# Attention values in one stationary block of high and low rows, halves added by VectorE; maximum as bias of one sequence's exponentials

## The chip, the cores and the metric

The kernel runs on one core of one Trainium2 chip. The metric is the device time of one execution in microseconds (us). The engines are TensorE (PE; its weight loads are PEld), VectorE (DVE), ScalarE (ACT), GpSimd (POOL) and SyncE (SP), which here issues the transfers. Each engine runs its own queue in order; they wait for each other by semaphores.

## The reference, cut to what matters

```python
# x: 32 sequences of 64 tokens, 1024 wide; 32 query heads, 8 key and value heads, 32 wide
x = x + attn(cond(x))          # cond: linear layer with a low-rank term chosen by labeler
x = x + ffn(cond2(x))          # two linear layers with routed low-rank terms
# in attn, for each sequence:
q, k, v = split(x @ w_qkv.T + b_qkv)
q, k = rope(q), rope(k)
scores = where(causal, q @ k.T / sqrt(32), -1e20)
out = softmax(scores) @ v      # this product is what the change is about
out = out @ w_o.T + b_o
```

## The kernel before, in words

The time has five stages: weights of the first two layers are folded into one (up to about 150 us), attention over all tokens (to about 610 us), folding for the second half, the output projection, and the feed-forward layers. The change is in the attention stage.

Products are made in fp32r, a rounded fp32, and every factor is split into a high part and a low remainder; a product is then high x high, high x low and low x high, three passes. ScalarE makes the high parts (`*_h`), VectorE or GpSimd the low parts (`*_l`).

Attention works on 16 units of 128 tokens, two sequences b = 0 and 1 of 64 tokens each. It is a pipeline of three: in step u TensorE projects unit u to q, k and v, makes the scores of unit v = u - 1, and multiplies probabilities and values of unit w = u - 2. `steps` writes steps 0 and 1 out, then a loop over u = 2 to 14, then steps 15, 16 (no projection any more) and 17 (values only). In step 16 the place of the projection is taken by `fold2.first(k)`, the first products of the next stage, each of which needs one more row of weights; ScalarE makes the high row (L1145), VectorE or GpSimd the low row (L1151). In step 17, `last_values`, it is `fold2.second`.

A step's projection is 24 groups (k, part), k = 0 to 7 and part = 0 to 2. Ahead of each group, the table `BESIDE` names work of the older units: `transpose_p` (probabilities turned, L952), `attend` (values, L967), `transpose_qk` (q and k turned, L924) and `scores` (L937). At the end the down product of the low-rank term is scaled by VectorE (`low_down`, L774), turned (L978), and split (L670, L849), and `up` (L984) adds it; behind `up` VectorE writes `qkv` (L860) and the next step begins.

On VectorE a step is: `probs_low` of sequence 0 (L745), four operations of the rotation (L740, two behind `rot_re`, two behind `rot_im`; GpSimd finishes each pair, L706 and L708), the low part of the values (L791), `probs_low` of sequence 1, low parts of q and k (L749, L810), values into their blocks (L820), and for each sequence mask, maximum and subtraction (`less_max`, L828, L830, L832). ScalarE makes the exponentials: 16 small ones with their sums for sequence 0 (L613), one large for sequence 1 (L615), which VectorE sums (L760). GpSimd scales them (L697). The scores of sequence 0 stand in PSUM banks 4 and 5 (`s_ps`), those of sequence 1 in banks 6 and 7 (`t_ps`), which the turned tiles use as well.

In `attend` one stationary tile is the block of four value heads, 128 columns, with zeros for the two heads that do not belong to the moving probabilities; high and low values are two tiles, `vb_h` and `vb_l`. Each sequence has a bank of its own for the result, and ScalarE copies it to `attn` (`values_out`, L601):

```python
for vv, pp in ((vb_h, pt_h), (vb_l, pt_h), (vb_h, pt_l)):
    if pp is pt_l:
        pe.wait_ge(pt_low, 2 * v + b + 1)
    for q in range(QUADS):
        for j in range(2):
            mm = pe.matmul(s_ps[:, b, ...], vv[:, b, q, j, :, :], pp[:, q, j, :, :], ...)   # 128 x 256
```

Of the kernel before, what the change touches and what calls it, by code (L numbers as in the profile page):

```python
# [22 lines left out]
ALU = mybir.AluOpType  # L23
# [416 lines left out]
def attention(nc, a, sem, keep, psum, ring, c_h, a_raw, index, fold1, fold2):  # L440
# [21 lines left out]
    vb_h, vb_l = (sb(n, [P, BPU, QUADS, 2, 4, HD], F32R) for n in ("vb_h", "vb_l"))  # L462
# [27 lines left out]
    v_high, v_low, vb_zero, vb_high, vb_low = (sem(n) for n in ("v_high", "v_low", "vb_zero", "vb_high", "vb_low"))  # L490
# [14 lines left out]
    def diag(vb, b, h):  # L505

        flat = vb[h * SEQ:(h + 1) * SEQ, b, :, :, :, :].rearrange("p q j c d -> p q (j c d)")
        return flat.rearrange("p q (m d) -> p q m d", d=HD)[:, :, h:h + 7:6, :]
# [83 lines left out]
    def scalar(act):  # L592
# [14 lines left out]
        def exp_scores(v, b, sums):  # L607

            act.wait_ge(s_sub, 2 * v + b + 1)
            if sums:  # L610
                for g in range(2):
                    for c in range(KVH):
                        last = act.activation(prob[:, 0, g, c, :], prob[:, 0, g, c, :], ACT.Exp, scale=SCALE, accum_out=ssum[:, 0, g, c:c + 1])  # L613
            else:
                last = act.activation(prob[:, b, :, :, :], prob[:, b, :, :, :], ACT.Exp, scale=SCALE)  # L615
            last.then_inc(s_exp, 1)

        def step(u, main, score, value, nxt):
# [6 lines left out]
            if value:  # L625
# [5 lines left out]
                values_out(w, 0)  # L631
# [4 lines left out]
                values_out(w, 1)  # L636
            if score:
# [12 lines left out]
                act.wait_ge(vb_zero, 2)  # L650
                need(act, pv_done, 2 * v)
                for b in range(BPU):
                    for h in range(2):
                        last = act.activation(diag(vb_h, b, h), v_hl[b * SEQ:(b + 1) * SEQ, 0, :, :, h, :].bitcast(F32), ACT.Copy)
# [29 lines left out]
    def gpsimd(pool):  # L684
# [46 lines left out]
        pool.memset(vb_h[:, :, :, :, :, :].bitcast(F32), 0.0).then_inc(vb_zero, 1)  # L731
        pool.memset(vb_l[:, :, :, :, :, :].bitcast(F32), 0.0).then_inc(vb_zero, 1)
        steps(pool, step)

    def vector(dve):
        def rotate(v, part):

            pairs = qkv[:, 0:QK].rearrange("p (h i two) -> p h i two", i=HD // 2, two=2)
            for n, (dst, table) in enumerate(((roped[:, :, :, part], (cos, sin)[part]), (rot_t[:, part, :, :], (sin, cos)[part]))):
                last = dve.tensor_tensor(dst, pairs[:, :, :, n], table[:, :].unsqueeze(1).to_broadcast([P, NH, HD // 2]), ALU.mult)  # L740
            last.then_inc((rot_re, rot_im)[part], 1)
# [1416 lines left out]
```

## Time and profile before

| | |
|---|---|
| median of 3 runs | 1169.55 us (1167.64 to 1171.43) |
| the profiled execution | 1169.91 us, span 1168.1 us |
| TensorE busy | 1140.2 us, 98% of the span |
| VectorE busy | 684.0 us, 59% |
| ScalarE busy | 409.5 us, 35% |
| GpSimd busy | 206.8 us, 18% |
| granted TensorE clock, mean | 0.994 of full speed |

The time of an execution is its span in the profile and a little around it. Busy shares are means over all stages; what counts for the change is the attention stage, and in it the order in which one step's waits end. Matmuls are pipelined: the start of one and of the next tell the pace, the duration shown for one is longer.

### The profile page before, as it was taken

What the parts mean: (1) busy time and instruction counts of PE and PEld (TensorE: products, weight loads), DVE (VectorE), ACT (ScalarE), POOL (GpSimd) and SP (SyncE); (2) the same over time, 40 slices, a digit from 0 to 9 for tenths busy, and PEclk for the clock granted to TensorE, in tenths of its full rate; (3) what the DMA queues carried; (4) which work ended last, traced back from release to release, by engine and by line L of the source; (5) the groups of instructions that cost most, each with busy time, mean ns of one, the idle gap of its engine ahead of it and who ended that gap; (6) DMA issues with size and microseconds to landing.
All of it is one profiled execution on the core that took longest, in us unless ns stands there. A gap on an engine that the chain in (4) does not pass through costs nothing.

```text
span 1168.1 us, 16980 instructions
## 1 busy us (share of the span) xinstructions
PE 1140.2 (98%) x6176; PEld 996.5 (85%) x6176; DVE 684.0 (59%) x1197; ACT 409.5 (35%) x1173; POOL 206.8 (18%) x133
## 2 busy tenths in 40 slices
PE   8999999999999999999988999999999999999998
PEld 6888888888888888888888999788888788888886
DVE  5312147788888888888893334332136766667664
ACT  5312124555555555555553333111123322222221
POOL 0000124333343333444361000000000000000000
PEclk9999999999999999999989999999999999999999
DMA  8020032111111111111142114473561333322212
GB/s 286 15 64 19 10 117 67 46 57 51 45 45 51 48 45 45 45 45 36 39 147 90 56 37 159 130 215 101 153 180 57 106 109 109 109 108 99 80 57 90
DMA packets 89763, 98.30 MB, mean 84 GB/s; under 512 B 7666, under 2 KB 73842, under 8 KB 89714
## 3 DMA queue, kind: packets, MB, share of 16 engines
q1 hardware_dynamic: 89714, 97.64, 25.8%
q8 instruction: 32, 0.52, 0.2%
q14 instruction: 17, 0.14, 0.0%
HBM read 72.45 MB, written 25.17 MB: 84 GB/s over the span
## 4 chain that ended last, share of the span: by engine, by line
PE 92%; DVE 3%; DMA 2%; ACT 1%; POOL 1%; issue 1%; SPq 0%; DVEq 0%; POOLq 0%
PE psum L905 23%; PE psum L1541 14%; PE psum L1849 13%; PE psum L280 12%; PE psum L1281 9%; PE psum L967 4%; PE psum L1910 4%; PE psum L1829 4%; PE psum L937 4%; PE psum L952 2%; PE psum L924 2%; PE psum L984 1%; DVE low L774 1%; DMA raw<-x_t_scratch 1%; PE psum L1896 0%
## 5 line engine op out<-in xcount | busy, mean ns | idle before, releaser
L905 PE MATMUL psum<-p_h,c_high_low 128*128 128x512 f32 (+1 forms) x768 | 196.3, 359 | 0.5 <-DVE qkv L860 0.5
L905 PEld LDWEIGHTS psum<-p_h,c_high_low 128*128 128x128 f32 x768 | 133.6, 188 | 13.3 <-issue 0.7
L280 PE MATMUL psum<-c_high_low,w_h 128*128 128x512 f32 x384 | 120.4, 399 | 5.7 <-ACT w_h L345 5.7
L1541 PE MATMUL psum<-ring,rows 128*128 128x512 f32 x528 | 123.7, 392 | 1.2 <-DVE t_plain L1257 1.2
L1541 PEld LDWEIGHTS psum<-ring,rows 128*128 128x128 f32 x528 | 98.8, 188 | 24.1 <-DVE t_plain L1257 2.5
L1281 PE MATMUL psum<-chunk,rows 128*128 128x384 f32 (+1 forms) x576 | 110.2, 347 | 4.8 <-DVE rows L1151 2.5
L1281 PEld LDWEIGHTS psum<-chunk,rows 128*128 128x128 f32 x576 | 104.3, 194 | 5.4 <-issue 5.4
L905 PE MATMUL psum<-p_l,c_high_low 128*128 128x512 f32 (+1 forms) x384 | 104.2, 366 | 0.0
L280 PEld LDWEIGHTS psum<-c_high_low,w_h 128*128 128x128 f32 x384 | 74.0, 193 | 22.5 <-issue 5.6
L697 POOL TENSOR_TENSOR prob<-prob,sinv 128x1024 f32<-128x1024 f32 x32 | 61.9, 1935 | 125.2 <-DVE sinv L767 125.2
L687 POOL TENSOR_TENSOR c_high_low<-ring_plain,c_high_low 128x512 fp32r<-128x512 f32 x32 | 41.4, 1292 | 236.6 <-PE psum L280 139.9
L613 ACT ACTIVATE prob<-prob 128x64 f32<-128x64 f32 x240 | 57.8, 242 | 67.6 <-DVE prob L832 67.6
L905 PE MATMUL psum<-end_h,c_high_low 128*128 128x320 f32 x256 | 76.1, 310 | 0.0
L280 PE MATMUL psum<-c_high_low,w_l 128*128 128x512 f32 x192 | 73.9, 391 | 0.0
L905 PEld LDWEIGHTS psum<-p_l,c_high_low 128*128 128x128 f32 x384 | 66.5, 190 | 6.2
L1849 PE MATMUL psum<-t_high,s_blocks 128*128 128x512 f32 x192 | 65.8, 405 | 0.0
L266 DVE TENSOR_TENSOR p_l<-psum,p_h 128x512 fp32r<-128x512 f32 (+1 forms) x24 | 14.2, 602 | 83.5 <-ACT p_h L254 42.7
L1501 DVE TENSOR_TENSOR ring<-ring_plain,ring 128x512 fp32r<-128x512 f32 x22 | 15.2, 690 | 74.8 <-ACT ring L1496 74.8
L1541 PE MATMUL psum<-at,rows 128*128 128x512 f32 x240 | 56.5, 391 | 0.0
L905 PEld LDWEIGHTS psum<-end_h,c_high_low 128*128 128x128 f32 x256 | 47.0, 188 | 8.6
L1541 PEld LDWEIGHTS psum<-at,rows 128*128 128x128 f32 x240 | 45.0, 188 | 9.8
L601 ACT ACTIVATE ring_plain<-psum 128x512 f32<-128x512 f32 x32 | 19.3, 603 | 89.4 <-PE psum L967 89.4
(173 smaller groups left out, 2261.4 us busy)
## 6 DMA issues: line engine op xcount, KB each, us to landing
ring_plain<-in_x_t SPq DMA_DIRECT2D x32, 256.0 KB, 2.7
attn_scratch<-ring_plain SPq DMA_DIRECT2D x16, 512.0 KB, 2.7
ring_plain<-attn_scratch SPq DMA_DIRECT2D x32, 256.0 KB, 4.0
raw<-x_t_scratch SPq DMA_DIRECT2D x16, 512.0 KB, 4.1
rest<-in_b_base SPq DMA_DIRECT2D x16, 512.0 KB, 4.1
out<-rest SPq DMA_DIRECT2D x16, 512.0 KB, 2.6
ring_plain<-in_wqkv_t SPq DMA_DIRECT2D x10, 512.0 KB, 6.1
a_raw<-in_lora_a SPq DMA_DIRECT2D x32, 128.0 KB, 2.0
```

The costliest lines, as they stand in the source:

```text
L280: mm = pe.matmul(to, stationary, moving, start=k == 0 and m == 0, stop=k == KT - 1 and last, skip_group_check=True)
L613: last = act.activation(prob[:, 0, g, c, :], prob[:, 0, g, c, :], ACT.Exp, scale=SCALE, accum_out=ssum[:, 0, g, c:c + 1])
L687: pool.tensor_tensor(x_l[:, ks(half), :], x_raw[:, ks(half), :], x_h[:, ks(half), :].bitcast(F32), ALU.subtract).then_inc(x_low, 1)
L697: pool.tensor_tensor(rows, rows, sinv[:, b, :, :].rearrange("p g c -> p (g c)").unsqueeze(2).to_broadcast([P, 2 * KVH, SEQ]), ALU.mult).th ...
L905: mm = pe.matmul(to, sx[:, k, :], moving(w, n, k), start=first, stop=False, skip_group_check=True)
L937: mm = pe.matmul(o, qq[:, b, cols, :].rearrange("p g t -> p (g t)"), kk[:, q, b, :, :].rearrange("p c t -> p (c t)"), start=n == 0, stop=n ...
L967: mm = pe.matmul(s_ps[:, b, q * 4 * SEQ:(q + 1) * 4 * SEQ], vv[:, b, q, j, :, :].rearrange("p c d -> p (c d)"), pp[:, q, j, :, :].rearrang ...
L1281: mm = pe.matmul(self.tile(n, width), stationary, moving, start=k == 0 and m == 0, stop=k == KT - 1 and m == 2, skip_group_check=True)
L1541: mm = pe.matmul(self.psum[:, self.BANK_OF[i], :], w[:, cols], s, start=m == 0 and p == 0, stop=m == KT - 1 and p == 2, skip_group_check=True)
L1829: mm = pe.matmul(self.gate_ps[:, u, :], s[:, k % HALF, :], self.room.gates[:, m, k, :], start=k == 0 and n == 0, stop=k == KT - 1 and n == ...
L1849: mm = pe.matmul(self.banks[self.BANK_OF[name]], s[:, k, :], w[:, k, :], start=name in ("p1", "p5", "p6") and k == 0 and n == 0, stop=k == ...
L1910: mm = pe.matmul(self.banks[{"c11": "a", "c12": "c", "c21": "b", "c22": "d"}[name]], self.zt[:, r, s, u, :], w[m], start=name == "c22" and ...
```

## The change

Values: one tile `vb` holds, for each group of two heads, 64 columns of high values and 64 of low ones. One pass with all 128 columns over `pt_h` writes high x high to PSUM rows 0 to 63 and low x high to rows 64 to 127; a second pass with the 64 high columns over `pt_l` adds to rows 0 to 63. No zero blocks for the other pair of heads are multiplied any more. ScalarE copies rows 64 to 127 to `beside`, and VectorE adds them to rows 0 to 63 and writes `attn`, in two operations, rows 0 to 63 and rows 64 to 127. The result now takes both banks of `s_ps`, so `attend` of sequence 1 waits for `pv_out` of sequence 0. Places: `values_out` stands on VectorE behind the third operation of the rotation, with `probs_low` of sequence 1 and then the fourth behind it; the second `values_out` ahead of the low parts of q and k.

Exponentials: in the full steps the maximum of sequence 0 is not subtracted by VectorE; it is multiplied by -SCALE (128 x 16) and given to ScalarE's exponentials as bias.

`BESIDE`: `transpose_qk` goes from (2, 1) to (3, 0) and from (3, 1) to (3, 2), `scores` from (4, 0) and (5, 0) to (4, 2) and (5, 2).

```diff
-    vb_h, vb_l = (sb(n, [P, BPU, QUADS, 2, 4, HD], F32R) for n in ("vb_h", "vb_l"))
+    vb = sb("vb", [P, BPU, QUADS, 2, 2, 2, HD], F32R)
+    beside = sb("beside", [SEQ, QUADS, 2, GRP * SEQ])
...
+    def values(rows):
+
+        return s_ps[rows, :, :].rearrange("p q (j t) -> p q j t", j=2)
+
+    high_rows, low_rows = slice(0, SEQ), slice(SEQ, P)
...
-        def values_out(w, b):
+        def values_beside(w, b):
             act.wait_ge(pv_done, 2 * w + b + 1)
-            if b == 0:
-                need(act, stored, 16 * w)
-            act.activation(attn[:, :, b, :], s_ps[:, b, :].rearrange("p (k t) -> p k t", k=KT), ACT.Copy).then_inc(pv_out, 1)
+            need(act, pv_out, 2 * w + b)
+            act.activation(beside[:, :, :, :], values(low_rows), ACT.Copy).then_inc(pv_beside, 1)
...
-                        last = act.activation(prob[:, 0, g, c, :], prob[:, 0, g, c, :], ACT.Exp, scale=SCALE, accum_out=ssum[:, 0, g, c:c + 1])
+                        last = act.activation(prob[:, 0, g, c, :], prob[:, 0, g, c, :], ACT.Exp, scale=SCALE, bias=smax[:, 0, g, c:c + 1],
+                                              accum_out=ssum[:, 0, g, c:c + 1])
...
+        def values_out(w, b):
+            dve.wait_ge(pv_beside, 2 * w + b + 1)
+            if b == 0:
+                need(dve, stored, 16 * w)
+            for j in range(2):
+                to = attn[j * SEQ:(j + 1) * SEQ, :, b, :].rearrange("p (q g) t -> p q g t", q=QUADS)
+                one, two = (t[:, :, j, :].rearrange("p q (g t) -> p q g t", g=GRP) for t in (values(high_rows), beside[:, :, :, :]))
+                last = dve.tensor_tensor(to, one, two, ALU.add)
+            last.then_inc(pv_out, 1)
...
-                rotate(v, 1)
+                rotate(v, 1, (0,))
+                if value:
+                    values_out(w, 0)
+                    probs_low(w, 1)
+                rotate(v, 1, (1,))
...
+            if value and not score:
+                values_out(w, 0)
+                probs_low(w, 1)
             if value:
-                probs_low(w, 1)
+                values_out(w, 1)
...
+                    if main and b == 0:
+                        dve.tensor_scalar(row(smax, b), row(smax, b), -SCALE, None, ALU.mult).then_inc(s_sub, 1)
+                        return
                     dve.tensor_tensor(flat(b), flat(b), row(smax, b).unsqueeze(2).to_broadcast([P, 2 * KVH, SEQ]), ALU.subtract).then_inc(s_sub, 1)
...
-            for vv, pp in ((vb_h, pt_h), (vb_l, pt_h), (vb_h, pt_l)):
+            else:
+                pe.wait_ge(pv_out, 2 * v + 1)
+            for parts, pp in ((2, pt_h), (1, pt_l)):
                 if pp is pt_l:
                     pe.wait_ge(pt_low, 2 * v + b + 1)
                 for q in range(QUADS):
                     for j in range(2):
+                        v_at = vb[:, b, q, j, 0:parts, :, :].rearrange("p m h d -> p (m h d)")
+                        mm = pe.matmul(s_ps[0:parts * SEQ, q, j * GRP * SEQ:(j + 1) * GRP * SEQ], v_at, pp[:, q, j, :, :].rearrange("p g t -> p (g t)"),
+                                       start=parts == 2 and j == 0, stop=parts == 1 and j == 1, skip_group_check=True)
...
-                  (2, 1): [(attend, 2, 1), (transpose_qk, 1, (0, 1))], (3, 1): [(transpose_qk, 1, (2,))],
+                  (2, 1): [(attend, 2, 1)], (3, 0): [(transpose_qk, 1, (0, 1))], (3, 2): [(transpose_qk, 1, (2,))],
```

What stands where, at three places. First VectorE in a full step, from `probs_low` of sequence 0 to the low parts of q, before the change (`pt_l`: low probabilities; `roped`, `rot_t`: rotation; `v_hl`: values; the names behind "waits" are semaphores):

```order
L745 TENSOR_TENSOR pt_l<-psum,pt_h 128x1024 [waits pt_high]
L740 TENSOR_TENSOR roped<-qkv,cos 128x640 [waits rotated,qk_t,const_in,qkv_out]
L740 TENSOR_TENSOR rot_t<-qkv,sin 128x640
L740 TENSOR_TENSOR roped<-qkv,sin 128x640
L740 TENSOR_TENSOR rot_t<-qkv,cos 128x640
L791 TENSOR_TENSOR v_hl<-qkv,v_hl 128x256 [waits v_high]
L745 TENSOR_TENSOR pt_l<-psum,pt_h 128x1024 [waits pt_high]
L749 TENSOR_TENSOR q_l<-psum,q_h 128x2x2x64 [waits qk_high]
```

The same place after the change, line numbers of the changed kernel (`ring_plain` is where `attn` lies):

```order
L753 TENSOR_TENSOR pt_l<-psum,pt_h 128x1024 [waits pt_high]
L747 TENSOR_TENSOR roped<-qkv,cos 128x640 [waits rotated,qk_t,const_in,qkv_out]
L747 TENSOR_TENSOR rot_t<-qkv,sin 128x640
L747 TENSOR_TENSOR roped<-qkv,sin 128x640
L763 TENSOR_TENSOR ring_plain<-psum,beside 64x8x64 [waits attn_stored,pv_beside]
L763 TENSOR_TENSOR ring_plain<-psum,beside 64x8x64
L753 TENSOR_TENSOR pt_l<-psum,pt_h 128x1024 [waits pt_high]
L747 TENSOR_TENSOR rot_t<-qkv,cos 128x640
L813 TENSOR_TENSOR v_hl<-qkv,v_hl 128x256 [waits v_high]
L763 TENSOR_TENSOR ring_plain<-psum,beside 64x8x64 [waits pv_beside]
L763 TENSOR_TENSOR ring_plain<-psum,beside 64x8x64
L767 TENSOR_TENSOR q_l<-psum,q_h 128x2x2x64 [waits qk_high]
```

The fourth operation of the rotation has moved behind two adds and the second `probs_low`, and two more adds stand ahead of `q_l`.

Second, TensorE in step 16, from the second `attend` to the second turn of q and k, before the change (L1281: products of the next stage):

```order
L967 MATMUL psum<-pt_h,vb_h 128x256 [waits pt_high]
L967 MATMUL psum<-pt_h,vb_h 128x256 x3
L967 MATMUL psum<-pt_h,vb_l 128x256 x4
L967 MATMUL psum<-pt_l,vb_h 128x256 [waits pt_low]
L967 MATMUL psum<-pt_l,vb_h 128x256 x3
L924 MATMUL psum<-ident,roped 128x128 [waits pt_low,rotated]
L924 MATMUL psum<-ident,roped 128x128 x7
L1281 MATMUL psum<-chunk,rows 128x392 [waits f2_row_low,f2_chunk_low]
L1281 MATMUL psum<-chunk,rows 128x392 x11
L924 MATMUL psum<-ident,roped 128x128 [waits qk_low]
```

And after it:

```order
L997 MATMUL psum<-pt_h,vb 128x256 [waits pv_out,pt_high]
L997 MATMUL psum<-pt_h,vb 128x256 x3
L997 MATMUL psum<-pt_l,vb 64x256 [waits pt_low]
L997 MATMUL psum<-pt_l,vb 64x256 x3
L1310 MATMUL psum<-chunk,rows 128x392 [waits f2_row_low,f2_chunk_low]
L1310 MATMUL psum<-chunk,rows 128x392 x11
L952 MATMUL psum<-ident,roped 128x128 [waits pt_low,rotated]
L952 MATMUL psum<-ident,roped 128x128 x7
L952 MATMUL psum<-ident,roped 128x128 [waits qk_low]
L952 MATMUL psum<-ident,roped 128x128
```

Both turns of q and k have moved behind the products that need the third row of weights.

Third, VectorE in step 16 behind the values' low part (`v_hl`), where the third and fourth rows of weights are split, before the change:

```order
L791 TENSOR_TENSOR v_hl<-qkv,v_hl 128x256 [waits v_high]
L745 TENSOR_TENSOR pt_l<-psum,pt_h 128x1024 [waits pt_high]
L1151 TENSOR_TENSOR rows<-rows_plain,rows 128x1024 [waits f2_row_low,f2_row_high]
L1151 TENSOR_TENSOR rows<-rows_plain,rows 128x1024 [waits f2_row_high]
L749 TENSOR_TENSOR q_l<-psum,q_h 128x2x2x64 [waits qk_high]
```

And after it:

```order
L813 TENSOR_TENSOR v_hl<-qkv,v_hl 128x256 [waits v_high]
L763 TENSOR_TENSOR ring_plain<-psum,beside 64x8x64 [waits pv_beside]
L763 TENSOR_TENSOR ring_plain<-psum,beside 64x8x64
L1180 TENSOR_TENSOR rows<-rows_plain,rows 128x1024 [waits f2_row_low,f2_row_high]
L1180 TENSOR_TENSOR rows<-rows_plain,rows 128x1024 [waits f2_row_high]
L767 TENSOR_TENSOR q_l<-psum,q_h 128x2x2x64 [waits qk_high]
```

The rows of weights now stand behind the adds of the second sequence. On ScalarE the copy for these adds stands behind the high parts of the same two rows, as `values_out` did.

## Rows read from the trace of the kernel before

**Rows 1.** Busy windows, core 0: length, busy time and count by engine, granted clock, DMA.

```profile
200.00:560.00 360.00, 357.21 (x2285) 321.67 (x2284) 294.69 (x431) 191.05 (x704) 149.34 (x92) 1.00 0.13 46
```

**Rows 2.** Timeline of TensorE, one step: start, duration, line, tiles, count, idle before.

```profile
305.60 1.03 PE L952 MATMUL psum<-ident,prob 128*128 128x128 f32 x8
...
308.65 0.64 PE L967 MATMUL psum<-pt_h,vb_h 128*128 128x256 f32 x4
309.12 0.63 PE L967 MATMUL psum<-pt_h,vb_l 128*128 128x256 f32 x4
...
315.39 1.04 PE L924 MATMUL psum<-ident,roped 128*128 128x128 f32 x8
...
320.13 0.28 PE L937 MATMUL psum<-k_h,q_h 128*128 128x256 f32 x1
...
323.76 0.27 PE L937 MATMUL psum<-k_h,q_h 128*128 128x256 f32 x1
...
332.40 0.98 PE L984 MATMUL psum<-pb,lows 128*128 128x512 f32 x4
333.22 1.04 PE L952 MATMUL psum<-ident,prob 128*128 128x128 f32 x8
```

**Rows 3.** Timeline of VectorE, the same step.

```profile
305.33 1.89 DVE L860 TENSOR_TENSOR qkv<-psum,b_bc 128x512 f32<-128x512 f32 x3 [0.30 <-PE psum L984]
...
310.34 0.82 DVE L740 TENSOR_TENSOR roped<-qkv,sin 128x640 f32<-128x640 f32 x1
311.07 2.23 DVE L740 TENSOR_TENSOR rot_t<-qkv,cos 128x640 f32<-128x640 f32 x1
...
313.56 1.21 DVE L745 TENSOR_TENSOR pt_l<-psum,pt_h 128x1024 fp32r<-128x1024 f32 x1
...
321.77 1.22 DVE L828 TENSOR_TENSOR prob<-psum,hidden 128x1024 f32<-128x1024 f32 x1 [1.06 <-PE psum L937]
...
330.19 0.59 DVE L774 TENSOR_SCALAR low<-psum 64x128 f32<-64x128 f32 x2 [0.42 <-PE psum L905]
330.81 1.22 DVE L760 TENSOR_REDUCE ssum<-prob 128x16 f32<-128x1024 f32 x1
```

**Rows 4.** Timeline of ScalarE and GpSimd, the same step.

```profile
310.35 0.60 ACT L601 ACTIVATE ring_plain<-psum 128x512 f32<-128x512 f32 x1 [2.35 <-PE psum L967]
310.50 2.12 POOL L706 TENSOR_TENSOR roped<-roped,rot_t 128x640 f32<-128x640 f32 x1 [1.59 <-DVE rot_t L740]
...
311.14 1.03 ACT L605 ACTIVATE pt_h<-psum 128x1024 fp32r<-128x1024 f32 x1 [0.19 <-PE psum L952]
...
313.38 1.71 POOL L708 TENSOR_TENSOR roped<-roped,rot_t 128x640 f32<-128x640 f32 x1 [0.76 <-DVE rot_t L740]
...
325.54 0.26 ACT L613 ACTIVATE prob<-prob 128x64 f32<-128x64 f32 x1 [4.46 <-DVE prob L832]
...
329.39 1.04 ACT L615 ACTIVATE prob<-prob 128x1024 f32<-128x1024 f32 x1
```

**Rows 5.** Timeline of step 16, each engine's rows in order of time.

```profile
584.82 3.93 PE L1281 MATMUL psum<-chunk,rows 128*128 128x392 f32 x12 [1.97 <-DVE rows L1151]
588.58 0.63 PE L967 MATMUL psum<-pt_h,vb_h 128*128 128x256 f32 x4
...
593.33 2.63 DVE L1151 TENSOR_TENSOR rows<-rows_plain,rows 128x1024 fp32r<-128x1024 f32 x2
...
594.43 1.04 PE L924 MATMUL psum<-ident,roped 128*128 128x128 f32 x8
...
595.13 0.38 ACT L640 ACTIVATE keys<-psum 128x256 f32<-128x256 f32 x1
595.23 2.40 PE L1281 MATMUL psum<-chunk,rows 128*128 128x392 f32 x12
...
608.10 6.60 PE L1281 MATMUL psum<-chunk,rows 128*128 128x392 f32 x27 [2.38 <-POOL rows L1151]
```

**Rows 6.** Busy window behind the first wait of step 16, core 0.

```profile
584.80:588.60 3.80, 3.79 (x13) 3.80 (x14) 3.80 (x3) 0.36 (x1) 2.41 (x1) 0.55 0.97 320
```

More of the change, by code:

```diff
@@ L630, in step @@
                         fold2.copy_out(act, i, 0, i)
-                values_out(w, 0)
+                values_beside(w, 0)
                 probs_high(w, 1)
@@ L635, in step @@
                     fold2.high_row(act, 3)
-                values_out(w, 1)
+                values_beside(w, 1)
             if score:
@@ L653, in step @@
                     for h in range(2):
-                        last = act.activation(diag(vb_h, b, h), v_hl[b * SEQ:(b + 1) * SEQ, 0, :, :, h, :].bitcast(F32), ACT.Copy)
+                        last = act.activation(diag(0, b, h), v_hl[b * SEQ:(b + 1) * SEQ, 0, :, :, h, :].bitcast(F32), ACT.Copy)
                 last.then_inc(vb_high, 1)
@@ L730, in gpsimd, with rotate @@
         pool.wait_ge(fold1.done, fold1.TILES * fold1.STEPS)
-        pool.memset(vb_h[:, :, :, :, :, :].bitcast(F32), 0.0).then_inc(vb_zero, 1)
-        pool.memset(vb_l[:, :, :, :, :, :].bitcast(F32), 0.0).then_inc(vb_zero, 1)
+        pool.memset(vb[:, :, :, :, :, :, :].bitcast(F32), 0.0).then_inc(vb_zero, 1)
         steps(pool, step)
     def vector(dve):
-        def rotate(v, part):
+        def rotate(v, part, which=(0, 1)):
             pairs = qkv[:, 0:QK].rearrange("p (h i two) -> p h i two", i=HD // 2, two=2)
             for n, (dst, table) in enumerate(((roped[:, :, :, part], (cos, sin)[part]), (rot_t[:, part, :, :], (sin, cos)[part]))):
+                if n not in which:
+                    continue
                 last = dve.tensor_tensor(dst, pairs[:, :, :, n], table[:, :].unsqueeze(1).to_broadcast([P, NH, HD // 2]), ALU.mult)
-            last.then_inc((rot_re, rot_im)[part], 1)
+            if 1 in which:
+                last.then_inc((rot_re, rot_im)[part], 1)
         def probs_low(w, b):
@@ L819, in step @@
                     for h in range(2):
-                        last = dve.tensor_copy(diag(vb_l, b, h), v_hl[b * SEQ:(b + 1) * SEQ, 1, :, :, h, :].bitcast(F32))
+                        last = dve.tensor_copy(diag(1, b, h), v_hl[b * SEQ:(b + 1) * SEQ, 1, :, :, h, :].bitcast(F32))
                 last.then_inc(vb_low, 1)
@@ L966, in attend @@
                     for j in range(2):
-                        mm = pe.matmul(s_ps[:, b, q * 4 * SEQ:(q + 1) * 4 * SEQ], vv[:, b, q, j, :, :].rearrange("p c d -> p (c d)"),
-                                       pp[:, q, j, :, :].rearrange("p g t -> p (g t)"), start=n == 0, stop=pp is pt_l and j == 1, skip_group_check=True)
-                        n += 1
+                        v_at = vb[:, b, q, j, 0:parts, :, :].rearrange("p m h d -> p (m h d)")
+                        mm = pe.matmul(s_ps[0:parts * SEQ, q, j * GRP * SEQ:(j + 1) * GRP * SEQ], v_at, pp[:, q, j, :, :].rearrange("p g t -> p (g t)"),
+                                       start=parts == 2 and j == 0, stop=parts == 1 and j == 1, skip_group_check=True)
             mm.then_inc(pv_done, 1)
```

14 lines of the change are left out of this document (6 added, 8 removed).

## The prediction

> **What bounds the kernel now.** I read the busy windows first: from 200 to 560 us, the loop over units, TensorE is busy 357.2 of 360 us at full granted clock, VectorE 294.7 [rows 1]. So TensorE sets the pace, with little room: anything it loses there is added to the time, but what it gains counts only as far as the other engines keep up. Then the timeline of one step. TensorE starts the transposes of the probabilities at 305.60 and again at 333.22: a step takes 27.62 us [rows 2]. All times below with a plus sign are counted from that start. At the end of the step stands a chain over other engines: second scores at 323.76, `less_max`, exponentials, the sum at 330.81, `lows`, and `up` at 332.40 [rows 2, 3]. There are 14 such steps (13 turns of the loop and step 15). One more place matters, step 16, where attention of the last units stands beside the first products of the next stage; there TensorE waits 2.0 and 2.4 us for rows of weights [rows 5].
>
> **What the change removes on TensorE.** Each `attend` has 12 matmuls of 256 columns now, 8 afterwards. Four of them follow each other in 0.47 us (308.65 to 309.12), so 0.119 each and 0.48 less per `attend` [rows 2]. 32 of these are 15.2 us, the most that there is to gain. The second pass has only 64 stationary columns, but streams the same 256 columns; I give it no gain.
>
> **What it adds in a step, first half.** The Scalar copy now takes 64 rows by 1024 columns from PSUM. The nearest row, 128 by 1024 from PSUM, took 1.03 us, the old copy 0.60 [rows 4]. The old copy began 1.70 after the first matmul of `attend` (308.65 to 310.35); with 0.48 less it begins at +4.27 and ends at +5.30. VectorE is free for the adds at +5.47, where the fourth rotation started (311.07) [rows 3], so the copy is just covered. Each add is 64 by 512 with one operand in PSUM. Three such operations of 128 by 512 took 1.89 us, which is 0.685 for one and 0.60 from start to start [rows 3]. The two 64-row operations of `low_down`, which write the lower rows and then the upper, took 0.59 together, double one: no overlap there [rows 3]. I take that for the adds too: 2 x 0.695 = 1.39 us, and the adds end at +6.86.
>
> The Trainium skill, page "VectorE: DVE Perf Modes", section on two Vector instructions with no wait between them, says the same as a rule: an instruction whose output starts in another group of 32 partitions starts only when all earlier ones are finished. By the overlapped spacing the sum would be 0.1 to 0.2 us less in a step; the `low_down` row agrees with the page.
>
> Then `probs_low` (1.14 to the next start, from 1.21 less the overlap) ends its place at +8.00. Now the fourth rotation. In the kernel before it takes 2.23 us against 0.82 for its three sisters, because GpSimd's addition (310.50, 2.12 us) runs beside it: it ends at 313.30, 0.68 after GpSimd's end at 312.62 [rows 3, 4]. `probs_low`, which reads PSUM, ran beside GpSimd at 313.56 undisturbed. So the adds fill the 1.4 us that were lost, and the moved rotation takes 0.82: end at +8.82. GpSimd's second addition ended 1.79 after the end of the rotation (315.09 against 313.30), so `rotated` comes at +10.61, and TensorE may go on at about +10.66. In the kernel before it was at the q and k transposes at +9.79.
>
> TensorE itself arrives there at 9.79 - 2 x 0.48 - 0.09 (it waited a moment for `pt_l` at the third pass) + 1.46 for the two groups of projection now ahead of it, that is +10.20; a group is about 0.73, from the three between the score blocks, 3.63 less 1.43 for the block itself. So it waits 0.46. The gain of 0.95 is already half gone, and the transposes start 0.87 later than before.
>
> **Second half of the step.** From these transposes to the first scores five groups and one small turn lie as before (315.39 to 320.13), and three groups between the score blocks as before (to 323.76): 8.37 together [rows 2]. The second scores start at 10.66 + 8.37 = +19.03; before +18.16. From there a chain runs that TensorE cannot shorten. VectorE starts on scores 1.64 after their first matmul (320.13 to 321.77). Mask, maximum and subtraction lead to the exponentials 3.77 later (321.77 to 325.54); these take 1.04 for the second sequence, which keeps its subtraction; 0.03 on, the sum starts, and from the sum to `up` it is 1.59 (330.81 to 332.40); `up` to the next step is 0.82 [rows 2 to 4]. Sum: 1.64 + 3.77 + 1.07 + 1.59 + 0.82 = 8.89. The step becomes 19.03 + 8.89 = 27.92, **0.30 longer** than 27.62.
>
> Why did this chain not bind before? It would give 18.16 + 8.89 = 27.05, under 27.62: VectorE was late for another reason, the subtraction for sequence 0 (about 1.2, as the mask of the same size) in front of mask 1, and `low_down` waiting for TensorE's last group. The change removes that subtraction: a 128 by 16 operation of about 0.25 (from the reciprocal of that size) stands there. But the second scores are two groups nearer the end of the step, so VectorE waits for TensorE about 0.8 us in front of mask 1 (the blocks are 3.63 apart, mask, maximum and the small operation take 2.8), and what was removed only lengthens this wait. The bias is read from SBUF by 16 exponentials that start later than before only by neighbours' shifts and end a microsecond ahead of need; cost nil, and if each took 0.06 more, 0.2 us of the step. 14 steps: **+4.2 us**. Bounds: if `rotated` is no limit, TensorE goes on at +10.20, the step is 27.46 and the term -2.2; if each add takes 0.82 like a rotation and the biased exponentials their 0.2, it is about +0.6 a step, +8.4.
>
> **Step 16.** `attend` 0 starts at 588.58. Copy from 589.80 to 590.83, adds to 592.25, `probs_low` to 593.47, then four matmuls: `attend` 1 is over at 594.05. In the kernel before VectorE was on the low row of weights 2 at 593.33, straight behind `probs_low` [rows 5]. Now `values_out` of sequence 1 stands ahead of it: copy 594.32 to 595.35, adds to 596.77, row 2 (1.2 to 1.3) to 598.0. TensorE's third row of products, at 595.23 before, starts at 598.1, having done nothing for 4.0 us. Ahead of it the q and k transposes were done; now they stand behind. And the clock: before, TensorE waited 1.97 us in its queue and the granted clock then was 0.55 of full over 584.8 to 588.6; twelve matmuls took 3.93 us there, 2.40 at 595.23 [rows 5, 6]. I expect the level of 1.2 GHz again behind the 4.0 us: end of the twelve about 601.85. Then the transposes, and the copy to `keys` 0.70 behind their start (594.43 to 595.13): 602.55 against 595.13, **+7.4 us**.
>
> The Trainium skill, page "TensorE: Matmul & The Clock Gate", Part 1, holds that an idle TensorE falls to 1.2 GHz and only activity frees the clock; the granted 0.55 agrees. Without that fall this term would be 5.9.
>
> From `keys` everything follows in queue order on ScalarE (queries, keys, values, row 4, three chunks, three rows) and behind it on GpSimd, for whose rows TensorE waited 2.38 us at 608.10 [rows 5]. There is no slack in between, so the end of step 16 moves by the same 7.4. Also both q and k turns now meet at k = 3 with nothing between: the last turn waits for `q_l`, about 1.1 us, inside these 7.4. In step 17 VectorE and GpSimd set the first `attend`; the second saves 0.48. Bounds for steps 16 and 17: 4 (no clock fall, a little shadow) to 8.
>
> **The sum** on the profiled execution, 1169.9 us (span 1168.1, the rest around it): +4.2 + 7.4 - 0.5 = 1181.0. The median of the runs is 0.4 below that execution, so I predict **1180.5 us**.
>
> **Rivals.**
> 1. *TensorE stays the bound* (chance 8 in 100, the one on the other side). If the chain behind the second scores were shorter than TensorE's own work there (1.43 + seven groups' worth and the rest, some 6.6 us to `up`, against 8.07 for the chain), and `rotated` 0.46 earlier, each step would save up to 0.95: -13.3. With 4 to 7 us lost in step 16 that is 1160 to 1163 us. It decides at a chain 1.4 us shorter; for it speaks TensorE's 99%, against it every duration in the chain.
> 2. *Only step 16 loses* (17 in 100): the adds are quicker than I think or start to start 0.60, `rotated` comes in time, the loop is between -0.16 and +0.1 a step: about 1174.5.
> 3. *Step 16 absorbs its delay* (10 in 100): the weight rows are made in idle time elsewhere and only the loop's 4.2 are left, or a small part of the 7.4: 1173.
> 4. *VectorE's queue is worse than walked* (7 in 100): adds slowed beside GpSimd, +0.6 or more a step: 1186 to 1190.
> My own case holds 58 in 100, 1176 to 1185.
>
> **Numbers.** A change under 0.3% (3.5 us) is what a measurement of this kernel can hardly tell from none. Slower than 1173.1 holds my case, rival 4, and most of 2 and half of 3: 0.78. Same, 1166 to 1173: 0.13. Faster: 0.09. The range 1171 to 1186 leaves out rival 1, a part of 4 and the low ends of 2 and 3, under 2 in 10.
>
> **What would show it.** In the profile after: `attend` of 8 matmuls in 0.95 us; the rotation that took 2.23 at 0.82; TensorE waiting for GpSimd's `roped` about 0.5 in each step; mask 1 waiting about 0.8 for the scores; TensorE waiting near 1.0 us for `low` and 0.5 for `lows`; steps of 27.9. In step 16 a wait of about 4 us ahead of the third row of products with a granted clock near 0.55 behind it. I am wrong if the steps take under 27.5, which would say that the chain at their end is shorter than my sum, or if the third row of products starts without that wait.

## The result, and the profile of the changed kernel

| | before | after | predicted |
|---|---|---|---|
| median | 1169.28 us (1167.64 to 1171.43, 4 runs) | 1196.33 us (1192.86 to 1196.87, 4 runs) | 1180.5 us, 1171 to 1186 |
| profiled span | 1168.1 us | 1194.1 us | |
| one step of the loop | 27.62 us | 29.01 us in the mean, 28.60 in most | 27.92 us |
| step 16, start of the transposes to the next | 34.55 us | 40.94 us | 7.4 us more |

The changed kernel is slower, ratio 1.0222 (1.0202 to 1.0242). The direction was right. The size was not: 27.1 us where 11.1 were predicted (1181.0 less 1169.9), above the range's end.

First the busy window of the loop and that of the stretch with step 16 (length, busy time and instructions of PE, PEld, DVE, ACT and POOL, granted clock, share and rate of DMA):

```profile
200.00:560.00 360.00, 334.98 (x2081) 298.25 (x2081) 284.96 (x463) 210.78 (x663) 140.20 (x86) 0.99 0.13 45
600.00:650.00 50.00, 34.69 (x191) 31.58 (x190) 37.43 (x52) 24.66 (x44) 25.02 (x13) 0.88 0.28 97
```

Before, TensorE was busy 357.2 of 360 us [rows 1]. Now it is 335.0, and no other engine is near full: the loop has become a chain through several engines. The granted clock of the loop is 0.99 where it was 1.00.

The timeline of TensorE in one step, from 253.71 to 282.31, so 28.60 us:

```profile
253.71 1.03 PE L980 MATMUL psum<-ident,prob 128*128 128x128 f32 x8
256.76 0.63 PE L997 MATMUL psum<-pt_h,vb 128*128 128x256 f32 x4
257.22 0.63 PE L997 MATMUL psum<-pt_l,vb 128*64 128x256 f32 x4
257.69 1.04 PE L980 MATMUL psum<-ident,prob 128*128 128x128 f32 x8
...
264.38 1.09 PE L952 MATMUL psum<-ident,roped 128*128 128x128 f32 x8 [0.35 <-POOL roped L714]
...
272.79 0.27 PE L965 MATMUL psum<-k_h,q_h 128*128 128x256 f32 x1
...
279.87 0.30 PE L1007 MATMUL psum<-ident,low 128*128 128x128 f32 x1 [1.57 <-DVE low L792]
281.51 0.97 PE L1013 MATMUL psum<-pb,lows 128*128 128x512 f32 x4 [0.17 <-DVE lows L877]
282.31 1.04 PE L980 MATMUL psum<-ident,prob 128*128 128x128 f32 x8
```

Read against [rows 2] from the start of each step: the q and k transposes stand at +10.67 (before +9.79), the second scores at +19.08 (+18.16). I had predicted +10.66 and +19.03. So two thirds of the step went as walked. The rest did not: TensorE waits 1.57 us for `low`, where 1.0 was predicted.

VectorE in the same step:

```profile
259.18 1.38 DVE L763 TENSOR_TENSOR ring_plain<-psum,beside 64x512 f32<-64x512 f32 x2
260.59 1.23 DVE L753 TENSOR_TENSOR pt_l<-psum,pt_h 128x1024 fp32r<-128x1024 f32 x1
261.73 0.82 DVE L747 TENSOR_TENSOR rot_t<-qkv,cos 128x640 f32<-128x640 f32 x1
...
273.31 0.17 DVE L858 TENSOR_SCALAR smax<-smax 128x16 f32<-128x16 f32 x1
274.41 1.22 DVE L853 TENSOR_TENSOR prob<-psum,hidden 128x1024 f32<-128x1024 f32 x1 [0.93 <-PE psum L965]
275.67 1.22 DVE L855 TENSOR_REDUCE smax<-prob 128x16 f32<-128x1024 f32 x1
276.92 1.23 DVE L860 TENSOR_TENSOR prob<-prob,smax 128x1024 f32<-128x1024 f32 x1
278.96 0.25 DVE L785 RECIPROCAL sinv<-ssum 128x16 f32<-128x16 f32 x1 [0.82 <-ACT prob L618]
279.13 0.59 DVE L792 TENSOR_SCALAR low<-psum 64x128 f32<-64x128 f32 x2
279.91 1.22 DVE L778 TENSOR_REDUCE ssum<-prob 128x16 f32<-128x1024 f32 x1 [0.19 <-ACT prob L621]
```

The second subtraction ends at 278.15, and then VectorE waits 0.82 us for the exponentials of sequence 0. That wait is what the prediction did not have. ScalarE shows why:

```profile
273.52 0.35 ACT L618 ACTIVATE prob<-prob,smax 128x64 f32<-128x64 f32 x1 [3.62 <-DVE smax L858]
...
278.84 1.04 ACT L621 ACTIVATE prob<-prob 128x1024 f32<-128x1024 f32 x1
```

The 16 exponentials fill 273.52 to 278.84, 5.32 us. In the kernel before, 325.54 to 329.39 is 3.85 [rows 4]. The group of all 240 of them, in the page of costliest groups, gives the price of one:

```profile
L618 ACT ACTIVATE prob<-prob,smax 128x64 f32<-128x64 f32 x240 | 80.0, 335 | 55.1 <-DVE smax L858 55.1
```

It was 242 ns before, so 0.093 us more for each, 1.5 for 16. By the predicted walk the exponential of sequence 1 would start at 19.03 + 1.64 + 3.77 = +24.44; it starts at +25.13. From there to the next step it is 3.47 us, and 3.48 had been predicted.

Step 16, each engine's rows in order of time:

```profile
604.69 2.36 PE L1310 MATMUL psum<-chunk,rows 128*128 128x392 f32 x12 [1.96 <-DVE rows L1180]
...
614.06 1.38 DVE L763 TENSOR_TENSOR ring_plain<-psum,beside 64x512 f32<-64x512 f32 x2 [0.75 <-ACT beside L606]
615.48 2.36 DVE L1180 TENSOR_TENSOR rows<-rows_plain,rows 128x1024 fp32r<-128x1024 f32 x2
616.85 4.21 PE L1310 MATMUL psum<-chunk,rows 128*128 128x392 f32 x12 [3.88 <-DVE rows L1180]
620.89 1.04 PE L952 MATMUL psum<-ident,roped 128*128 128x128 f32 x8
621.53 0.39 ACT L646 ACTIVATE keys<-psum 128x256 f32<-128x256 f32 x1 [7.50 <-PE psum L952]
```

The wait of 3.88 us ahead of the third row of products is there (4.0 predicted), and behind it twelve matmuls take 4.21 us where full clock gives 2.40 [rows 5]. The granted clock of that stretch:

```profile
616.85:620.90 4.05, 4.05 (x13) 3.96 (x14) 0.99 (x1) 0.00 (x0) 0.00 (x0) 0.50 0.19 76
```

`keys` comes at +19.84 from the start of the step, before at +13.31, so 6.5 later.

One thing in the loop is new. In four of its steps the transposes at the start take nearly double, here with the end of the step before and with the granted clock of that stretch:

```profile
308.54 0.30 PE L1007 MATMUL psum<-ident,low 128*128 128x128 f32 x1 [1.58 <-DVE low L792]
...
310.18 1.60 PE L1013 MATMUL psum<-pb,lows 128*128 128x512 f32 x4 [0.17 <-DVE lows L877]
311.58 1.91 PE L980 MATMUL psum<-ident,prob 128*128 128x128 f32 x8
```

```profile
311.60:313.50 1.90, 1.90 (x10) 1.90 (x10) 1.25 (x3) 0.00 (x0) 1.90 (x2) 0.50 0.01 3
```

0.50 is the level of 1.2 GHz. It follows a wait of 1.58 us for `low`, but the same wait stands in every step, and only every fourth shows it. Of the fourteen steps, 195.49 to 601.69 is 406.2 us; fourteen at 28.62 would be 400.7, so these falls cost 5.5 us.

The span's 26.0 us more are thus: 14 x 0.98 = 13.7 for the undisturbed step (28.60 against 27.62), some 5.8 with the clock and rounding up to the loop's 19.5, 6.4 for step 16, 0.3 before the loop, and -0.3 behind step 16.

### The profile page after: what moved, and what is told of

It is laid out like the page before. It is cut to its first block, busy times and chain, and to the rows that moved or that the text cites. A ratio compares the mean times of both kernels' runs of the same rounds, so it can differ in the third digit from the quotient of the medians.

```text
span 1194.1 us, 16835 instructions
## 1 busy us (share of the span) xinstructions
PE 1132.9 (95%) x6048; PEld 985.0 (82%) x6048; DVE 690.8 (58%) x1261; ACT 445.3 (37%) x1173; POOL 205.2 (17%) x132
## 4 chain that ended last, share of the span: by engine, by line
PE 68%; DVE 10%; ACT 10%; POOL 5%; issue 4%; DMA 2%; SPq 0%; DVEq 0%; POOLq 0%
PE psum L1570 14%; PE psum L280 12%; PE psum L1878 12%; PE psum L1310 9%; ACT prob L618 7%; PE psum L933 7%; PE psum L1939 4%; PE psum L1858 4%; POOL roped L712 2%; POOL roped L714 2%; PE psum L965 2%; PE psum L952 2%; DVE ssum L778 2%; PE psum L980 2%; DVE prob L853 2%
## 5 line engine op out<-in xcount | busy, mean ns | idle before, releaser
L933 PE MATMUL psum<-p_h,c_high_low 128*128 128x512 f32 (+1 forms) x768 | 199.5, 363 | 0.5 <-DVE qkv L888 0.5
L933 PEld LDWEIGHTS psum<-p_h,c_high_low 128*128 128x128 f32 x768 | 133.1, 189 | 13.7 <-issue 0.7
L618 ACT ACTIVATE prob<-prob,smax 128x64 f32<-128x64 f32 x240 | 80.0, 335 | 55.1 <-DVE smax L858 55.1
L606 ACT ACTIVATE beside<-psum 64x1024 f32<-64x1024 f32 x32 | 32.8, 1025 | 70.7 <-PE psum L997 70.6
L853 DVE TENSOR_TENSOR prob<-psum,hidden 128x1024 f32<-128x1024 f32 x32 | 39.1, 1223 | 30.5 <-PE psum L965 30.5
```

The source lines that it names most:

```text
L606: act.activation(beside[:, :, :, :], values(low_rows), ACT.Copy).then_inc(pv_beside, 1)
L853: dve.tensor_tensor(flat(b), scores, hidden[:, :].unsqueeze(1).to_broadcast([P, 2 * KVH, SEQ]), ALU.add).then_inc(s_masked, 1)
L933: mm = pe.matmul(to, sx[:, k, :], moving(w, n, k), start=first, stop=False, skip_group_check=True)
```

## Experiments

One table for all of them, from the profiled executions: the mean step (transposes of the first step to those of step 16, over 14), step 16, and what lies behind it. The ratio is against runs of the kernel before that were taken side by side with the kernel in question; their median went from 1167.97 to 1169.83. The last column goes from 548.7 to 554.5, though the edits touch only its beginning, so single executions compare only to some 3 us, and the argument goes by the steps.

| kernel | median, us | ratio to before (95%) | step | step 16 | behind |
|---|---|---|---|---|---|
| before | 1169.28 | | 27.62 | 34.55 | 551.7 |
| after | 1196.33 | 1.0222 (1.0202 to 1.0242) | 29.01 | 40.94 | 551.5 |
| after, no bias | 1187.20 | 1.0148 (1.0124 to 1.0171) | 28.21 | 41.29 | 554.5 |
| before, bias alone | 1169.24 | 1.0005 (0.9992 to 1.0018) | 27.70 | 33.49 | 548.7 |
| after, old table | 1187.22 | 1.0160 (1.0137 to 1.0184) | 28.61 | 36.86 | 552.2 |
| before, constant pointer | 1187.19 | 1.0152 (1.0128 to 1.0176) | 28.75 | 34.53 | 551.7 |
| after, old step 16 | 1190.73 | 1.0198 (1.0174 to 1.0222) | 28.85 | 37.67 | 550.9 |
| after, addition on VectorE | 1187.59 | 1.0166 (1.0145 to 1.0186) | 28.16 | 41.17 | 552.3 |
| before, sum behind `lows` | 1169.71 | 1.0008 (0.9995 to 1.0021) | 27.72 | 33.90 | 548.7 |
| combination | 1172.02 | 1.0027 (1.0016 to 1.0038) | 27.72 | 37.24 | 551.1 |
| and values' low half on GpSimd | 1168.96 | 1.0008 (0.9994 to 1.0022) | 27.53 | 36.25 | 551.4 |
| and `low_down` first | 1173.28 | 1.0042 (1.0027 to 1.0057) | 27.85 | 36.78 | 551.7 |
| the same with the bias | 1173.99 | 1.0043 (1.0027 to 1.0059) | 27.85 | 36.95 | 550.6 |

My theory after the result: the pointer operand makes each exponential 0.093 us longer, so that in the side by side kernel they and not VectorE end last. The rival: the 0.7 us come from the new places in TensorE's queue or from the adds.

**After, no bias.** The subtraction of sequence 0 is back.

```diff
-prob[:, 0, g, c, :], ACT.Exp, scale=SCALE, bias=smax[:, 0, g, c:c + 1], accum_out=...
+prob[:, 0, g, c, :], ACT.Exp, scale=SCALE, accum_out=...
-                    if main and b == 0:
-                        dve.tensor_scalar(row(smax, b), row(smax, b), -SCALE, None, ALU.mult)...
-                        return
```

> The changed kernel with the maximum of sequence 0 subtracted by VectorE again and no bias. Theory (the 16 biased exponentials, 0.335 us each against 0.242, end 0.7 us after the second subtraction and hold the chain to up; the longer idle time then costs clock in every fourth step): the exponentials take 0.242, steps about 28.2 us instead of 29.0 in the mean, no step with a fallen clock, median about 1184.5 us. Rival (the exponentials are hidden, the new places of scores and of the q and k transposes cost the time): steps stay near 28.6 to 29, median 1194 to 1197.

A step takes 28.21 us, and no step shows a fallen clock. The total came out 2.7 us above the expected 1184.5, about as much as the stretch behind step 16 was longer in the profiled execution (554.5 against 551.5). VectorE and ScalarE at the end of one (it begins at 251.56):

```profile
274.84 1.23 DVE L856 TENSOR_TENSOR prob<-prob,smax 128x1024 f32<-128x1024 f32 x1
276.43 0.25 DVE L784 RECIPROCAL sinv<-ssum 128x16 f32<-128x16 f32 x1 [0.36 <-ACT prob L618]
...
276.30 1.04 ACT L620 ACTIVATE prob<-prob 128x1024 f32<-128x1024 f32 x1
```

The exponential of sequence 1 now starts at +24.74, 0.39 sooner than with the bias, and the step is 0.39 shorter. So the bias made a step longer although it takes 1.05 us from VectorE. Even here the 16 exponentials end 0.23 behind the second subtraction (276.07): they start a subtraction later, at +20.89.

**Before, bias alone.** The same edit the other way round, on the kernel before.

> The kernel before with the bias alone. Theory: the exponentials take 0.335 (1.5 us more), but the subtraction that VectorE saves (1.2 us) comes ahead of them, so in the old places the step grows only by about 0.1 us, median 1169 to 1173. Rival (the bias costs its 0.7 us a step wherever it stands): steps 28.3, median about 1179.

No difference. The exponentials take 335 ns there as well, but in a kernel whose TensorE is busy all the time the chain is covered: 0.08 us a step.

**Before, constant pointer.** The exponentials of the kernel before read a column of zeros as their bias and the subtraction stays, so that nothing is saved and only the pointer is added.

```diff
-prob[:, 0, g, c, :], ACT.Exp, scale=SCALE, accum_out=...
+prob[:, 0, g, c, :], ACT.Exp, scale=SCALE, bias=hidden[:, 0:1], accum_out=...
```

> The kernel before, subtraction kept, whose 16 exponentials read a constant column of zeros as bias (same result). Theory: it is reading a bias from SBUF at all that costs: 0.335 us each, with nothing saved on VectorE, so steps near 28.8, median about 1186 (more if the clock falls). Rival (what costs is a column just written, or another one for each exponential): 0.242 each and 1169 us.

Its group of exponentials:

```profile
L613 ACT ACTIVATE prob<-prob,hidden 128x64 f32<-128x64 f32 x240 | 79.9, 334 | 67.7 <-DVE prob L832 67.7
```

334 ns with a constant column that nobody writes in the loop: what costs is the operand, not a wait for `smax`. And 1.5 us more of exponentials make a step 1.13 longer.

The Trainium skill, page "ScalarE: Activation LUTs", in the section on what ACT_TABLE_LOAD costs, gives the same size: about 93 ns for each pointer operand of one column. The rows agree: 242 ns without, 334 and 335 with.

**After, old table.** TensorE's queue has the table of before.

> The changed kernel with the table of places of before. Theory: the chain from the rotation to the first scores sets the loop, so TensorE waits about 1.9 us at the q and k transposes instead of 0.5 there, and steps stay near 28.6; step 16 gives back about 6 us; median 1185 to 1191, by whether the clock still falls. Rival (the places are what costs in the loop): steps near 27.7, median below 1178.

The step is 28.61, the undisturbed step of the changed kernel: apart from the falls of the clock the places in the table are worth nothing in the loop. TensorE waits elsewhere:

```profile
263.57 1.09 PE L952 MATMUL psum<-ident,roped 128*128 128x128 f32 x8 [1.79 <-POOL roped L714]
279.17 0.30 PE L1007 MATMUL psum<-ident,low 128*128 128x128 f32 x1 [0.20 <-DVE low L792]
```

1.79 us for GpSimd's `roped` and 0.20 for `low`, where it was 0.35 and 1.57; the sum is nearly the same, 1.99 and 1.92. The chain through the other engines sets the step, wherever in it TensorE stands and waits. With this split the clock does not fall in the loop. That, and step 16, 4.1 us shorter (6 expected), is why the total is 9 us less. Step 16 of this run, where only TensorE's table is the old one and VectorE still makes the addition ahead of row 2:

```profile
609.34 1.97 PE L952 MATMUL psum<-ident,roped 128*128 128x128 f32 x8 [1.81 <-POOL roped L714]
610.03 2.36 DVE L1180 TENSOR_TENSOR rows<-rows_plain,rows 128x1024 fp32r<-128x1024 f32 x2
611.40 2.94 PE L1310 MATMUL psum<-chunk,rows 128*128 128x392 f32 x12
```

While VectorE adds and then makes row 2, TensorE waits for `roped` and turns q and k, and no wait of 3.9 us is left.

**After, old step 16.** The old table and the old order of VectorE, rows of weights 2 and 3 ahead of the addition of sequence 1, in step 16 alone.

```diff
-            if value:
+            if value and (main or not score):
                 values_out(w, 1)
             if score and not main:
                 fold2.low_row(dve, 2, after_other=True)
                 fold2.low_row(dve, 3)
+                values_out(w, 1)
```

> The changed kernel, with the old order of step 16 alone put back: there the old table of TensorE's queue, and the rows of weights 2 and 3 on VectorE ahead of the addition of the halves of sequence 1. My theory (the addition in front of row 2 makes TensorE wait 3.9 us and run twelve matmuls at the low clock): step 16 loses its 6 to 7 us, total 1189 to 1191. Rival (step 16 is longer for what its own attends and additions cost, wherever they stand): 1194 to 1196.

The total came out at 1190.7 as expected, but not for the reason given. Step 16 gained 3.3 us, half of what I gave it, and less than the 4.1 of the old table alone; 2.3 came from the loop, where two steps show a fallen clock at their start instead of four. What is left of step 16:

```profile
612.05 1.97 PE L953 MATMUL psum<-ident,roped 128*128 128x128 f32 x8 [1.81 <-POOL roped L714]
613.67 4.27 PE L1314 MATMUL psum<-chunk,rows 128*128 128x392 f32 x12
```

The transposes start 0.5 later than before (+13.10 against +12.61), but behind a wait of 1.81 us that was not there, and they and the twelve matmuls take 1.97 and 4.27 us instead of 1.04 and 2.40. So in the old places `roped`, late by the adds, costs a fall of the clock as well. Set beside the run with the old table, VectorE's old order gained nothing: the twelve matmuls start 1.62 behind the transposes instead of 2.06, but take 4.27 instead of 2.94, because the clock came back later. The old order of VectorE with the new table was not run.

**After, addition on VectorE.** GpSimd's second addition of the rotation is moved to VectorE.

```diff
-                pool.wait_ge(rot_im, v + 1)
-                pool.tensor_tensor(roped[:, :, :, 1], roped[:, :, :, 1], rot_t[:, 1, :, :], ALU.add)...
+                dve.wait_ge(rot_im, v + 1)
+                dve.tensor_tensor(roped[:, :, :, 1], roped[:, :, :, 1], rot_t[:, 1, :, :], ALU.add)...
```

> The changed kernel, with the second addition of the rotation (1.8 us on GpSimd) done by VectorE, about 0.8 us there. My theory (in the first half of a step TensorE waits for GpSimd's addition, and its delay is carried to the end of the step): rotated comes about 1 us earlier, TensorE's wait for it goes, a step takes 28.1 to 28.2 instead of 28.6, total 1189 to 1191, and 1184 to 1186 if the falls of the clock go too. Rival (VectorE has no room, and what GpSimd loses VectorE pays): no change, 1195 to 1198.

It takes 0.83 us there, and TensorE comes to the transposes at +10.21 without a wait, the +10.20 predicted for its own arrival. The step is 28.16 in the mean and 28.13 in most; the clock of the profiled execution is low only at the start of the first step (eight transposes in 1.45, step 28.54), though TensorE still waits 1.57 us for `low` in each step. The total lies between the two values expected.

**Before, sum behind `lows`.** The kernel before with the sum of sequence 1 one place later in VectorE's queue.

> The kernel before, with only the sum for sequence 1 moved behind the low halves of the values in VectorE's queue. Theory: TensorE is the bound there, the chain at the end of its step is nearly hidden, so a step gains at most 0.1 us: 1167.5 to 1169.3. Rival (the end chain bound before, too): steps of 27.0 to 27.2, 1161 to 1164.

Nothing is gained (27.72 a step): the end chain is hidden in the kernel before, as the prediction had it.

**The combination.** No bias, the addition on VectorE, the sum behind `lows`, the old step 16, on the changed kernel.

> Side by side without the bias (all subtractions back), the second addition of the rotation on VectorE, the sum for sequence 1 moved behind the low halves of the values (lows) in VectorE's queue, and the old order in step 16. If the places named so far are all that keeps the 8-matmul attends from paying, a step takes 27.3 to 27.4 and the total is 1163 to 1167, below the kernel before. Rival (TensorE's own 27.1 or so a step cannot be reached, the end chain stays as it is): steps of 27.7 to 27.9 and 1170 to 1174.

27.72 a step: the rival was right, and the reason is VectorE, busy 321.4 us of the window 200 to 560 where it was 294.7 [rows 1].

```profile
322.71 1.22 DVE L853 TENSOR_TENSOR prob<-psum,hidden 128x1024 f32<-128x1024 f32 x1 [1.14 <-PE psum L961]
...
328.88 1.23 DVE L857 TENSOR_TENSOR prob<-prob,smax 128x1024 f32<-128x1024 f32 x1
330.46 0.25 DVE L782 RECIPROCAL sinv<-ssum 128x16 f32<-128x16 f32 x1 [0.36 <-ACT prob L618]
330.64 0.59 DVE L789 TENSOR_SCALAR low<-psum 64x128 f32<-64x128 f32 x2
```

From the first mask (322.71) to the next step (333.39) is a chain of 10.7 us, six operations of VectorE in a row first. What TensorE saves cannot shorten it. Against the undisturbed 28.60 the step is 0.88 shorter, and the two edits measured alone, the bias (0.39) and the addition on VectorE (0.47), give 0.86 of that: the place of the sum gave nothing that can be seen.

**Values' low half on GpSimd.** One more operation off VectorE, and the scores one group earlier.

> The last combination (no bias, second addition of the rotation on VectorE, sum for sequence 1 behind lows, old order in step 16) with the low half of the values (one subtraction of 0.42 us) moved from VectorE to GpSimd, which is idle for 8.9 us there, and both score blocks one group of projection (0.73 us) earlier on TensorE. Theory: in the last combination a step of 27.73 is set by the scores, by six VectorE operations behind them (7.4 us without a gap) and by the chain to up; then the step follows the scores: 27.0 to 27.1, total 1162 to 1165, below the kernel before. Rival: the operands of the first scores (k_l, q_l) are not ready earlier, or GpSimd's subtraction holds VectorE up as its addition did: steps of 27.4 to 27.7, 1168 to 1172.

Only 0.2 us of the 0.7 came: the scores, at +15.14 instead of +15.39, wait for `q_l`, which VectorE ends late.

```profile
319.83 0.39 PE L961 MATMUL psum<-k_h,q_h 128*128 128x256 f32 x1 [0.28 <-DVE q_l L767]
```

This is the best of the side by side kernels, and it is level with the kernel before, 1.0008 (0.9994 to 1.0022).

**`low_down` first, and the same with the bias.** `low_down` stands ahead of the reciprocal of sequence 0.

> The kernel of the run before (steps of 27.52 us), with low_down ahead of the reciprocal of sequence 0 in VectorE's queue, so that it no longer stands behind the 16 exponentials. Theory: the chain from the first mask to the end of the step (10.7 us) binds, TensorE waits 0.41 for low in it; this goes, but the exponential of sequence 1 (to +25.5) keeps lows from coming more than 0.3 earlier: steps of 27.2 to 27.3, total 1164 to 1166.5. Rival (another wait of the same size stands behind it, the normalised probabilities from GpSimd for the next transposes): steps of 27.4 to 27.5, 1168 to 1169.

> The same, but with the bias put back for sequence 0: VectorE loses 1.22 us of subtraction and gains 0.17. By the price of the pointer (0.093 us for each of 16) the exponentials start at about +19.6 and end at +25.0, that of sequence 1 at +26.0, 0.4 later than without the bias: steps 0.3 to 0.5 longer than without it, total 4 to 7 us more. Rival (where VectorE is the bound the lighter VectorE pays for it): steps shorter by up to 1.0, total up to 14 us less.

Both take 27.85 a step, and both expectations were wrong. Without the bias the step became 0.3 longer, and the bias then cost nothing. One row shows why, VectorE with `low_down` first:

```profile
330.51 0.59 DVE L792 TENSOR_SCALAR low<-psum 64x128 f32<-64x128 f32 x2 [0.31 <-PE psum L930]
```

`low_down` waits for TensorE's last group, and the reciprocal comes behind it at +25.47 in both (+24.61 in the run before). GpSimd's two multiplications with the reciprocals come later with it. The first (331.46 to 333.37) ends just ahead of the next transposes (333.50), which start 0.95 behind `up` instead of 0.69; the profile names no engine for that gap, so that they waited for GpSimd is read from the times alone. The second multiplication now runs beside VectorE's first rotation:

```profile
307.96 1.91 POOL L702 TENSOR_TENSOR prob<-prob,sinv 128x1024 f32<-128x1024 f32 x1
308.99 1.57 DVE L747 TENSOR_TENSOR roped<-qkv,cos 128x640 f32<-128x640 f32 x1
```

That rotation took 0.92 in the run before. `q_l` and with it the first scores come 0.28 later (+15.42), `up` gains back 0.21 behind them, and the transposes lose 0.26: together the 0.33 by which the step grew. The bias costs nothing there because its exponentials end at +25.21, ahead of the reciprocal's +25.47.

## Why the prediction was wrong

**The step that failed** is the one that put the bias at "cost nil, and if each took 0.06 more, 0.2 us of the step". Measured is 0.093 for each, 1.49 for the 16. By the walk they would start at about +19.8 and have until +24.44, where the second subtraction ends; at 0.242 each they end at +23.7, at 0.334 at +25.1. So 0.8 us of cover (the time by which they may grow before anything waits for them) stood against 1.5 us of cost, and 0.69 went into each step. The sentence spoke of a microsecond of cover, and that was about right; the error was to bound the price at 0.06, which for 16 is 0.96 and hardly more than the cover. No row was given for the 0.06. The trace of the kernel before has two rows that speak against it, copies of one shape from SBUF to SBUF, the first with a column (`hmask`) as its scale and the second with none:

```profile
L646 ACT ACTIVATE k_h<-keys,hmask 128x256 fp32r<-128x256 f32 x64 | 27.5, 525 | 0.0
L624 ACT ACTIVATE v_hl<-qkv 128x256 fp32r<-128x256 f32 x16 | 6.5, 408 | 1.5 <-DVE qkv L860 1.5
```

They are 0.117 apart; the tiles differ too, so this is only an estimate of the price, but at twice the 0.06 it is far outside the cover. The constant pointer in the kernel before shows the price, and the run without the bias shows what it did to the step: 0.39, since the returning subtraction starts the exponentials later and takes 0.3 of the gain.

On the profiled executions, 1195.9 against 1181.0, the forecast was 14.9 us too low. Fourteen times 0.68 (28.60 less 27.92) is 9.5 of these, the clock in the loop 5.5, step 16 takes 1.0 off, and the rest is rounding and the stretches outside.

**The clock in the loop** was not in the sum: 5.5 us in the profiled execution. TensorE's wait for `low` grew from the predicted 1.0 to 1.57. The falls within the loop went away without the bias, with the old table and with the addition on VectorE; but the run with the old table still has the bias, and in the last of the three the wait was the same 1.57. So the bias alone does not cause them, nor does that wait alone, and what decides which wait is followed by a fall stays open.

**What held.** `attend` in 0.93 us (0.95 predicted). The adds 1.38 (1.39), without overlap. The moved rotation 0.82 instead of 2.23. `rotated` at +10.62 (+10.61), TensorE's wait for it 0.35 (0.46). Second scores at +19.08 (+19.03), mask 1 waiting 0.93 for them (0.8). From the exponential of sequence 1 to the next step 3.47 (3.48). The +0.30 of a step was right for all but the exponentials: 28.60 less 0.69 is 27.91. No kernel was measured that has the 27.92 itself.

**Step 16** was +6.4 against +7.4. The mechanism, VectorE's addition ahead of row 2, a wait of 4 us and the low clock behind it, is in the rows; from `attend` of sequence 0 to `keys` it is 14.64 us where the kernel before had 6.55, 8.1 more and not 7.4. The total came near by luck: the first row of products ran at full clock this time, 2.36 us against 3.93 [rows 5], which I had taken as fixed, and that gave 1.6 back. Why it kept its clock is not shown. The cause was also told too simply. The remark that "there is no slack" held for the delay, but the addition ahead of row 2 makes TensorE wait 3.9 us only because the new table leaves it nothing to do meanwhile: with the old table alone 4.1 of the 6.4 us are gone, and VectorE's old order on top of it gained nothing. Of the 2.3 that are left the rows show a part, the wait of 1.8 for `roped`, late by the adds, and the low clock behind it.

**The rivals.** TensorE did not stay the bound (rival 1), step 16 was not alone (2) and did not absorb its delay (3). A step that is 0.6 or more longer, rival 4, came true (0.98), but by ScalarE's exponentials, not by VectorE's queue: each add took its predicted time.

**The swap as a whole.** Saving four matmuls in each `attend` saves TensorE 0.95 us a step and gives VectorE 2.76 us of adds, of which the quicker rotation returns 1.4. With the bias taken out and the queues rearranged, six edits brought a step back to 27.53, and the total to that of the kernel before and no further. In this best kernel the first mask stands at +16.86, later than before (+16.17), and the chain of 10.7 us through VectorE, ScalarE and TensorE follows it whatever TensorE saves. Whether another order would get the mask earlier was not tried.

## What to carry to other kernels

A column read as bias was a cost of each exponential here. Before calling such an operand free, look for a row that has one, multiply its price by the number of instructions in the chain, and set that against the cover. Sixteen small exponentials at 0.093 more each (1.49 us) cost more than the subtraction that they replaced (1.22). Where an engine is 99% busy, work taken from it counts only until the next chain, so add up that chain first; and work moved behind a wait may slow TensorE's clock as well as delay it.

## What the runs showed of the hardware

- An ACTIVATE of 128 by 64 takes 242 to 243 ns with no pointer operand and 334 to 335 with one, whether the column is written in each step or constant; the READ_ACCUMULATOR behind each stayed at 187 to 188.
- A copy from PSUM of 64 rows by 1024 takes 1.02 to 1.03 us, as long as one of 128 rows: half the rows save nothing.
- VectorE's rotation with both tensors in SBUF takes 2.23 us where it runs beside GpSimd's addition [rows 3, 4] and 0.82 away from it; the first rotation took 1.57 beside GpSimd's multiplication and 0.92 where that was nearly over.
- The granted clock fell to 0.50 in the loop behind some waits of 1.6 us and not behind others of the same length.
